# Expert results added into one DRAM row per token by accumulating scatters, instead of two stored rows per token added on chip

## The reference, cut to what matters

```python
def _L2_ffn_ref(x, Wr, br, W1, b1, W2, b2):       # x is the layer-normalised input
    logits = xt @ Wr + br
    w, idx = jax.lax.top_k(softmax(logits), 2)
    w = w / clip(sum(w), 1e-9)
    comb = zeros((T, E)).at[arange(T)[:, None], idx].add(w)
    h = gelu(einsum('td,edh->teh', xt, W1) + b1)
    o = einsum('teh,eho->teo', h, W2) + b2
    return xt + einsum('teo,te->to', o, comb)

x = x + tanh(g_ffn[2]) * _L2_ffn_ref(layernorm(x), ...)
```

## Time and profile before

| | us |
|---|---|
| median of 3 runs (2075.76 to 2081.41) | 2077.06 |
| profiled execution | 2073.58 |
| its span | 2071.5 |

### The profile page before, as it was taken

How to read it: one execution, slowest core, us unless ns; L and a number is a source line. 1 busy time by engine, 2 the same in 40 slices (tenths; PEclk the granted TensorE clock), 3 DMA queues, 4 the chain that set the end, 5 groups by cost and what they waited for, 6 DMA issues and landing times. The chain is left out here.

```text
span 2071.5 us, 31898 instructions
## 1 busy us (share of the span) xinstructions
PE 1722.6 (83%) x10297; PEld 1305.7 (63%) x10297; DVE 1167.2 (56%) x2517; ACT 888.8 (43%) x1828; POOL 331.8 (16%) x362
## 2 busy tenths in 40 slices
PE   6888468897579997879999839999962899969998
PEld 4444224556457665658888729999962788855446
DVE  4544546776435546778888472322227788861115
ACT  2222357766343220245555235555543555533222
POOL 1000000000000000420000044555545111001110
PEclk9998699999879998979999559999985899998999
DMA  4000100000300000100000751222233000010002
GB/s 140 1 0 0 41 0 1 1 1 1 109 1 1 1 1 8 28 1 1 1 1 1 276 185 62 72 70 72 72 121 113 1 1 1 1 44 0 0 1 82
DMA packets 63446, 78.44 MB, mean 38 GB/s; under 512 B 13999, under 2 KB 53194, under 8 KB 62935
## 3 DMA queue, kind: packets, MB, share of 16 engines
q1 hardware_dynamic: 49351, 50.43, 7.4%
q0 software_dynamic: 7584, 20.72, 3.0%
q10 hardware_dynamic: 6384, 5.58, 0.8%
HBM read 57.96 MB, written 18.74 MB: 37 GB/s over the span
## 5 line engine op out<-in xcount | busy, mean ns | idle before, releaser
L2556 PEld LDWEIGHTS moe_bank<-moe_xt,moe_w1e 128*128 128x128 f32 x1264 | 156.6, 195 | 5.9 <-DVE moe_xt L2414 1.9
L2556 PE MATMUL moe_bank<-moe_xt,moe_w1e 128*128 128x128 f32 x1264 | 157.5, 279 | 1.1 <-DVE moe_xt L2414 1.1
L2566 PE MATMUL moe_bank<-moe_w,moe_xin 128*128 x632 | 149.7, 380 | 0.0
L2617 ACT ACTIVATE moe_xin<-moe_bank,moe_b 128x128 f32<-128x128 f32 x316 | 90.5, 368 | 127.1 <-PE moe_bank L2556 127.0
L356 PE MATMUL l0f_hb<-l0f_xt,l0f_w 128*128 128x512 f32 x256 | 123.5, 613 | 5.6 <-DVE l0f_a L287 3.8
L935 POOL TENSOR_TENSOR all_x<-all_x,l1f_bias 128x256 f32 x32 | 23.1, 724 | 647.7 <-DVE l1f_xn L170 647.7
L2566 PEld LDWEIGHTS moe_bank<-moe_w,moe_xin 128*128 128x128 f32 x632 | 114.4, 191 | 12.4
L175 DVE BATCH_NORM_STATS2 all_stats<-all_x 128x6 f32<-128x256 f32 (+1 forms) x256 | 105.7, 422 | 21.4 <-DMA all_x<-in_x 3.0
L2423 DVE TENSOR_TENSOR moe_y<-moe_bank,moe_b2r 128x256 f32<-128x256 f32 x79 | 33.5, 424 | 119.8 <-PE moe_bank L2566 119.8
L2483 POOL DMA_INDIRECT moe_results<-moe_y,moe_row x79 | 78.0, 988 | 127.5 <-DVE moe_y L2423 124.2
L2414 DVE COPY moe_xt<-moe_bank 128x256 f32<-128x256 f32 x79 | 33.5, 425 | 108.0 <-PE moe_bank L2544 108.0
(11 more groups left out here) (457 smaller groups left out, 3894.1 us busy)
## 6 DMA issues: line engine op xcount, KB each, us to landing
moe_w<-in_L_ffn_W SPq DMA_DIRECT2D x32, 512.0 KB
moe_w<-moe_results SPq DMA_DIRECT2D x16, 512.0 KB, 8.7
all_x<-in_x SPq DMA_DIRECT2D x4, 1024.0 KB, 13.2
out_x<-all_x SPq DMA_DIRECT2D x8, 512.0 KB, 2.9
l0f_w<-in_L_ffn_w_T SPq DMA_DIRECT2D x2, 1024.0 KB
moe_inputs<-moe_xin ACTq DMA_DIRECT2D x16, 128.0 KB, 5.7
moe_inputs<-moe_w1e ACTq DMA_DIRECT2D x16, 128.0 KB, 5.1
moe_b2r<-in_L_ffn_b SPq DMA_DIRECT2D x1, 2048.0 KB, 12.2
```

Of the source, the lines that this page charges most:

```text
L2556: ins = nc.tensor.matmul(out, w1e[:, at:at + P], xt[:, u, c * P:(c + 1) * P], start=(c == 0), stop=(c == DC - 1))
L2566: ins = nc.tensor.matmul(bank[4 + u][:, 0:D], ht[:, u, c * P:(c + 1) * P], w2[:, ds(e * (HC * D) + c * D, D)], start=(c == 0), stop=(c == ...
L2617: ins = nc.scalar.activation(ht[:, u, m * P:(m + 1) * P], bank[1 + u][:, m * P:(m + 1) * P], ACT.Gelu, bias=b1[:, ds(e * HC + m, 1)])
```

## The change

`ys` is replaced by `sums`, with one row for each token and 128 spare rows that all unfilled slots share. Every expert tile is weighted before it leaves the chip and is added to the row of its token by a scatter that accumulates in DRAM.

- Before the router VectorE fills `zero` and makes `keep` and `keep_b`; `residual` runs in the router loop, one tile behind `norm`, and ScalarE's queue stores each new x tile to `sums` (`store_x`), and the zeros to the spare rows.
- The two routing weights of each token, already times tg, are stored behind its normalised row: `xnd` has rows of 258 values. The store of the weights is one transfer on ScalarE's queue of 4096 pieces of two values, right behind the sigmoids.
- The inverted list also gives which choice a slot is (`pick`), by three more operations on 128x79. A gather brings the row and both weights; VectorE makes the slot's weight from them in two one-column operations, and scales the tile after the bias by a second 128x256 operation.
- Store t waits until store t-1 has landed, since two tiles can hold the same token.
- At the end eight transfers of 512 KB load x from `sums`, and VectorE takes the statistics. The scaling on ScalarE, the addition on GpSimd and the addition on VectorE are gone.
- The load of the biases waits for the stores to `sums` as well, since `zero` lies in its place, and so does the first gather, together with the weights' store.

```diff
-        tgw = s.sb("tgw", [P, TOP, T])
+        xnd = nc.dram_tensor("moe_inputs", (B * S, ROW), F32, kind="Internal").ap()   # ROW = D + TOP
+        sums = nc.dram_tensor("moe_sums", (B * S + P, D), F32, kind="Internal").ap()
...
@ SyncE
                 sp.wait_ge(s.ranked, 1)
+                sp.wait_ge(s.sums_set, 16 * (T + 1))
                 sp.dma_start(b2r[:, :], ...).then_inc(s.b2_loaded, 16)
                 for q in range(T // QT):
-                    for k in range(TOP):
-                        at = (k * T + q * QT) * P
-                        sp.dma_start(results[:, k, q * QT:(q + 1) * QT, :],
-                                     ys[at:at + QT * P, :].rearrange("(t p) d -> p t d", p=P)).then_inc(results_loaded[k][q], 16)
+                    sp.dma_start(sh.x[:, q * QT * D:(q + 1) * QT * D].rearrange("p (t d) -> p t d", d=D),
+                                 sums[q * QT * P:(q + 1) * QT * P, :].rearrange("(t p) d -> p t d", p=P)).then_inc(x_loaded[q], 16)
...
@ VectorE
                 c = norm_vector(nc, dve, sh, s)
+                nc.vector.memset(zero, 0.0).then_inc(s.zero_set, 1)
+                c.link(nc.vector.tensor_scalar(keep[:, :], sh.rstd[:, :], tg, 1.0, ALU.mult, ALU.add))
+                c.link(nc.vector.tensor_scalar(keep_b[:, :], sh.shift[:, :], tg, None, ALU.mult))
...
-                unrolled(T, [(norm, 6), (best, 0)])
+                unrolled(T, [(norm, 6), (residual, 5), (best, 0)])
...
-                nc.vector.tensor_scalar(keep[:, :], sh.rstd[:, :], tg, 1.0, ALU.mult, ALU.add)
-                c.link(nc.vector.tensor_scalar(keep_b[:, :], sh.shift[:, :], tg, None, ALU.mult))
+                dve.wait_ge(s.wt_ready, 2)
+                nc.vector.tensor_scalar(wt[:, :, :], wt[:, :, :], tg, None, ALU.mult).then_inc(s.wt_ready, 1)
...
+                c.link(nc.vector.tensor_scalar(pick[:, 1, :], kt, float(T), None, ALU.is_gt))
+                c.link(nc.vector.tensor_scalar(pick[:, 0, :], pick[:, 1, :], -1.0, 1.0, ALU.mult, ALU.add))
+                c.link(nc.vector.scalar_tensor_tensor(kt, pick[:, 1, :], -float(T), kt, ALU.mult, ALU.add))
...
 copy_x:
+                    both = gathered(t)[:, D:ROW]
+                    nc.vector.tensor_scalar(part_w[:, t % NX:t % NX + 1], both[:, 0:1], pick[:, 0, t:t + 1], None, ALU.mult).then_inc(s.weight_step, 1)
                     nc.vector.tensor_copy(xt[:, u, :], bank[3 * u][:, 0:D]).then_inc(s.et_ready, 1)
+                    dve.wait_ge(s.weight_step, 2 * t + 1)
+                    nc.vector.scalar_tensor_tensor(tile_w[:, t % NX:t % NX + 1], both[:, 1:2], pick[:, 1, t:t + 1], part_w[:, t % NX:t % NX + 1],
+                                                   ALU.mult, ALU.add).then_inc(s.weight_step, 1)
 result:
-                    nc.vector.tensor_tensor(y[:, u, :], bank[4 + u][:, 0:D], b2r[:, ds(e * D, D)], ALU.add).then_inc(s.y_ready, 1)
+                    nc.vector.tensor_tensor(y[:, u, :], bank[4 + u][:, 0:D], b2r[:, ds(e * D, D)], ALU.add).then_inc(s.biased, 1)
+                    dve.wait_ge(s.biased, t + 1)
+                    nc.vector.tensor_scalar(y[:, u, :], y[:, u, :], tile_w[:, t % NX:t % NX + 1], None, ALU.mult).then_inc(s.y_ready, 1)
...
-                unrolled(T, [(add, 1), (stats, 0)])
+                for t in range(T):
+                    if t % QT == 0:
+                        dve.wait_ge(x_loaded[t // QT], 16)
+                    tile_stats(nc, sh, t).then_inc(s.stats_ready, 1)
...
@ GpSimd
                 pool.wait_ge(s.rows_ready, 1)
+                pool.wait_ge(s.sums_set, 16 * (T + 1))
+                pool.wait_ge(s.wt_stored, 16)
 gather:
                     if t >= NX:
                         pool.wait_ge(s.et_ps, t - NX + 1)
+                        pool.wait_ge(s.weight_step, 2 * (t - NX + 1))
 store:
                     pool.wait_ge(s.y_ready, t + 1)
-                    nc.gpsimd.indirect_dma_start(out=ys, out_offset=bass.IndirectOffsetOnAxis(ap=row[:, t:t + 1], axis=0),
-                                                 in_=y[:, u, :], in_offset=None).then_inc(y_stored[u], 16)
+                    if t >= 1:
+                        pool.wait_ge(y_stored[1 - u], 16 * ((t + 1) // 2))
+                    nc.gpsimd.indirect_dma_start(out=sums, out_offset=bass.IndirectOffsetOnAxis(ap=row[:, t:t + 1], axis=0),
+                                                 in_=y[:, u, :], in_offset=None, compute_op=ALU.add).then_inc(y_stored[u], 16)
...
-                for t in range(T):
-                    pool.wait_ge(s.scaled, t + 1)
-                    nc.gpsimd.tensor_tensor(x_tile(sh, t), x_tile(sh, t), results[:, 0, t, :], ALU.add).then_inc(s.summed, 1)
...
@ ScalarE
+                act.wait_ge(s.zero_set, 1)
+                act.dma_start(sums[B * S:B * S + P, :], zero).then_inc(s.sums_set, 16)
-                unrolled(T, [(copy, 0), (store, 1)])
+                unrolled(T, [(copy, 0), (store, 1), (store_x, 0)])
...
+                act.wait_ge(s.wt_ready, 3)
+                act.dma_start(xnd.rearrange("(t p) d -> p t d", p=P)[:, :, D:ROW], wt[:, :, :]).then_inc(s.wt_stored, 16)
...
-                for t in range(T):
-                    if t % QT == 0:
-                        act.wait_ge(results_loaded[0][t // QT], 16)
-                    nc.scalar.activation(results[:, 0, t, :], results[:, 0, t, :], ACT.Copy, scale=tgw[:, 0, t:t + 1]).then_inc(s.scaled, 1)
```

More of the change, by code:

```diff
@@ L2228, in stage_l2_ffn @@
     KT = TOP * T
-    RES = TOP * B * S
+    ROW = D + TOP
     NX, XN, GR, QT = 4, 16, 4, 4
@@ L2239, in stage_l2_ffn @@
         b2r = s.sb("b2r", [P, EXPERTS * D])
-        xin = s.sb("xin", [P, 2 * NX * D])
-        ht = xin[:, NX * D:2 * NX * D].rearrange("p (u h) -> p u h", u=2)
+        xin = s.sb("xin", [P, 2 * NX * ROW])
+        ht = xin[:, NX * ROW:NX * ROW + 2 * HID].rearrange("p (u h) -> p u h", u=2)
         xt = s.sb("xt", [P, 2, D])
@@ L2268, in stage_l2_ffn @@
         spare, found = s.sb("spare", [P, ET]), s.sb("found", [P, 2 * ET])
+        pick = s.sb("pick", [P, TOP, ET])
+        part_w, tile_w = s.sb("part_w", [P, NX]), s.sb("tile_w", [P, NX])
+        zero = b2r[:, (TOP + 5) * EXPERTS * T:(TOP + 5) * EXPERTS * T + D]
         row, token = s.sb("row", [P, ET], U32), s.sb("token", [P, ET], U32)
-        results = w1[:, :].rearrange("p (k t d) -> p k t d", k=TOP, d=D)
-        xnd = nc.dram_tensor("moe_inputs", (B * S, D), F32, kind="Internal").ap()
-        ys = nc.dram_tensor("moe_results", (RES + ET * P, D), F32, kind="Internal").ap()
+        xnd = nc.dram_tensor("moe_inputs", (B * S, ROW), F32, kind="Internal").ap()
+        sums = nc.dram_tensor("moe_sums", (B * S + P, D), F32, kind="Internal").ap()
         bank = [s.ps(f"bank{k}", [P, 512]) for k in range(8)]
@@ L2276, in stage_l2_ffn @@
                   "part_ready", "code_ready", "inv_ps", "rows_ready", "w1e_ready", "et_ps", "et_ready", "h_ps", "ht_ready", "y_ps",
-                  "y_ready", "y_stored0", "y_stored1", "kept", "scaled", "summed", "x_ready", "stats_ready"]:
+                  "y_ready", "biased", "weight_step", "y_stored0", "y_stored1", "kept", "sums_set", "wt_stored", "zero_set", "stats_ready"]:
             s[n] = s.sem(n)
@@ L2280, in stage_l2_ffn @@
         xs_loaded = [s.sem(f"xs_loaded{k}") for k in range(NX)]
-        results_loaded = [[s.sem(f"results_loaded{k}_{q}") for q in range(T // QT)] for k in range(TOP)]
+        x_loaded = [s.sem(f"x_loaded{q}") for q in range(T // QT)]
         y_stored = (s.y_stored0, s.y_stored1)
@@ L2287, in xn @@
             k = t % XN
-            return xin[:, k * D:(k + 1) * D] if k < 2 * NX else w1e[:, (k - 2 * NX) * D:(k - 2 * NX + 1) * D]
+            return xin[:, k * ROW:k * ROW + D] if k < 2 * NX else w1e[:, (k - 2 * NX) * D:(k - 2 * NX + 1) * D]
         def gathered(t):
-            return xin[:, (t % NX) * D:(t % NX + 1) * D]
+            return xin[:, (t % NX) * ROW:(t % NX + 1) * ROW]
         with nc.Block() as block:
@@ L2325, in norm, with residual @@
                     normalise(nc, sh, xn(t), t).then_inc(s.xn_ready, 1)
+                def residual(t, u):
+                    dve.wait_ge(s.xn_ready, t + 1)
+                    nc.vector.tensor_scalar(x_tile(sh, t), x_tile(sh, t), keep[:, t:t + 1], keep_b[:, t:t + 1],
+                                            ALU.mult, ALU.add).then_inc(s.kept, 1)
                 def best(t, u):
@@ L2422, in result @@
                     dve.wait_ge(s.y_ps, t + 1)
-                    nc.vector.tensor_tensor(y[:, u, :], bank[4 + u][:, 0:D], b2r[:, ds(e * D, D)], ALU.add).then_inc(s.y_ready, 1)
[L2425 to L2440, removed]
+                    nc.vector.tensor_tensor(y[:, u, :], bank[4 + u][:, 0:D], b2r[:, ds(e * D, D)], ALU.add).then_inc(s.biased, 1)
+                    dve.wait_ge(s.biased, t + 1)
+                    nc.vector.tensor_scalar(y[:, u, :], y[:, u, :], tile_w[:, t % NX:t % NX + 1], None, ALU.mult).then_inc(s.y_ready, 1)
+                unrolled(ET, [(copy_x, 2), (result, 0)])
```

(9 more changed lines are left out.)

14 lines of the change are left out of this document (4 added, 10 removed).

## The result

| | before | after |
|---|---|---|
| median of 4 runs each, us | 2076.41 (2075.26 to 2081.41) | 2162.18 (2159.77 to 2163.34) |
| profiled execution, us | 2073.58 | 2162.9 |
| its span | 2071.5 | 2161.1 |

What follows compares the result with a forecast made beforehand. TensorE was taken to bound router and expert tiles, with 34.0 us after them on the path; -19.2 + 3.0 + 0.7 + 0.8 + 1 + 5 = -8.7 us gave 2064.9, as median 2068 us; range 2058 to 2130.

Steps and rivals of the forecast that it cites:

- X: Expert loop: extra time of an accumulating store over a plain one, taken as 0.8 us, between bounds 0 and 2.7.
- Reading and writing overlap in both rows: Accumulating store: the reason given for an estimate nearer to the plain scatter, 0.8 us within 0.4 to 1.2.
- The wake: Expert loop: GpSimd starts 0.28 us after VectorE's end, so 0.25 us was added to a plain store's 2.44, giving 2.7.
- the cover for X: Expert loop: the store chain stays hidden under TensorE's 3.73 us a tile until X = 3.73 - 2.7 = 1.0 us.
- Rival 1: Expert loop: the chain of stores sets the pace; 2122 us at X = 1.7, near 2200 at 2.7; chance 0.35.
- ScalarE's queue: Router: 33 more transfers of 128 KB, issuing 0.33 us each and hidden; 1 us charged for the xn ring's last tiles.
- The sign by which the prediction called itself wrong: Expert loop: an accumulating store landing later than about 3.5 us after its start; 3.2 us was expected.
- The cover that I named: Router: the xn ring allows about eleven tiles, 13 us, against a queue landing that may grow to 12 or so.
- The weights' store: Before the ranking: ScalarE stands at the issue of 4096 pieces of 8 bytes; 5 us charged, between 0.33 and 22.
- The end: After the last expert store: half the bytes return and VectorE only measures; 34.0 us becomes 14.75, 19.2 us gained.
- keep and the zero fill: Before the router: with keep_b, they stand ahead of the first normalisation and put 0.7 us on the path.
- the three 128x79 operations: Behind the ranking: three more linked operations of 0.24 us with small gaps, costing 0.8 us.

Runs made afterwards that it cites:

- the two runs with the old pace: Changed kernel with a plain, non-accumulating scatter: 2074.31 us; changed kernel with odd tiles accumulating into a second, unread tensor, each store waiting two back: 2074.54 us.

## Why the prediction was wrong

1. **The accumulating store, X.** The failed step. X was taken as 0.8 us, with parts that gave 0.4 to 1.2; it is 1.36. Two parts were too small: the time on the transfer engines grew by 0.78 and not by 0.39, since the store is made of three times the packets and takes three times the time, not twice, and GpSimd's own part grew by 0.65, where I allowed 0.5 at most. The bounds 0 to 2.7 held it; the estimate inside them did not. "Reading and writing overlap in both rows" was no reason to lean to the plain scatter: the rows give a duration and a landing, and show no overlap.
2. **The wake.** Also failed. I put 0.25 us for GpSimd's waking, read from a wait for VectorE; after a landing it is 0.73 (plain store) and 0.86 us (accumulating). The plain chain is 3.16 us and not 2.7, so the cover for X was 3.73 - 3.16 = 0.57 us and not 1.0. With both, the chain is 4.66 instead of 3.5; 0.56 us of the difference is X and 0.61 the wake.
3. **Rival 1** is what happened, and its price of 76 us for each us over TensorE's pace is right: 76 x (4.66 - 3.73) = 71 us, and 14.9 us from the twelve long steps make 86 of the 90.2. Its times for a given X were too low, as it held the wake fixed: at the measured X of 1.36 it gives 2068 + 0.36 x 76 = 2095. Most of the way from there to 2162 is the wake, 0.61 x 76 = 46 us, the long steps with 15 us, which the prediction had nowhere, and ScalarE's queue with 11 us. The sign by which the prediction called itself wrong, a landing later than 3.5 us, showed (3.9). At chance 0.35 it was the second case; the two numbers that decide between it and the forecast were both estimates, and the range should have gone further towards the bound.
4. **ScalarE's queue.** Wrong by size: 1 us charged, 11.7 measured. The landing of about 12 us was foreseen. What failed is "issuing is 0.33 us each, hidden": with twice the bytes on this queue beside the weights an issue takes 0.6 us, and ScalarE's own next copy waits for two of them. The cover that I named, eleven slots of the xn ring, was not the one in use.
5. **The weights' store.** Wrong by size: 5 us charged, none measured. The issue of 4096 small pieces took 0.378 us; they landed 18.7 us later, near the 22 of the working, and nobody waited.
6. **The end.** Right, within 2 us. From the last store to the last statistics the prediction has 2.44 + 0.8 + 14.75 = 18.0 us, 18.4 less than before; measured are 19.7, 16.7 less. The landing is 3.80 instead of 3.24 us, and request to last statistics 15.9 instead of 14.75. (The other 2.2 of the 3.0 us lost are the last store's later start, which the table counts to the loop.)
7. **Small terms.** keep and the zero fill 1.0 with the rest of the router (0.7 predicted); the three 128x79 operations within 0.5 (0.8 predicted); the residual nothing, as the router without the stores of x shows, and the one-column operations and the second 128x256 operation nothing a tile, as the two runs with the old pace show.

## What to carry to other kernels

Before a transfer is put into a chain in which each waits for the one before, add up the whole period: issue on the engine, landing, and the waking of that engine after a transfer, read from a wait of that same kind. Here the transfer engines were a third busy and the chain with its late landings still cost 86 us. Ask which pairs really conflict: waiting only for these gave back 73 us. And an issue that costs 0.33 us beside a full stream doesn't keep that price when its queue is given twice the bytes: here it became 0.6 us, and the copies of the same engine stood behind it.

## What I had not expected of the hardware

- An accumulating scatter of 128 rows of 1 KB lands after 3.8 to 3.9 us and occupies GpSimd for 1.6 us; a plain one 2.4 and 0.99 us. With rows of 512 bytes it lands after 3.3 us and still occupies GpSimd for 1.59.
- After the landing of a store GpSimd starts the next indirect transfer 0.73 to 0.86 us later, after VectorE's end 0.28 us later. VectorE, waiting for the same landing, starts 0.60 us ahead of it. Why GpSimd takes longer is open.
- The accumulating store is made of 141 packets, with rows of 1 KB and of 512 bytes alike, where the plain one has 48; its engine time is about 1.17 and 0.75 us, where the plain one has 0.39.
- A store of 4096 pieces of 8 bytes cost its queue 0.378 us at the issue.
- Twelve of 78 steps of the chain took 5.3 to 6.9 us instead of 4.66. In eleven of them a transfer of an "instruction" queue of the profile starts while the store is under way, and the store lands up to 1.5 us late. Whether it is the cause is left open.
